# A third high-part buffer, split expert loads and a split down product in a fused time-mix and mixture-of-experts kernel

## The reference

```python
x = x + attn_ref(layernorm(x), ...)       # T = 2048 rows, H = 512
#   v = xln @ Wv; r = sigmoid(mix @ Wr); vmix = sum_t v*dec; x2 = x + r*(vmix @ Wo + bo)
#   kc = square(relu(shift(xc) @ Wck)); vc = kc @ Wcv; out = x2 + sigmoid(xc @ Wcr) * vc
x = x + ffn_ref(layernorm(x), ...)
#   scores = sigmoid(h @ gate_w); group-limited top 4 of 32 experts; weights normalised, times 2.5
#   up = einsum('th,ehi->tei', h, Wu); act = square(relu(up))          # EI = 256
#   routed = einsum('tei,te,eih->th', act, combine, Wd)
#   shared = square(relu(h @ Wsu)) @ Wsd                               # SI = 1024
```

## Time and profile before

| | |
|---|---|
| runs | 1074.92, 1075.74, 1079.47 us; median 1075.74 |
| profiled execution | 1076.93 us, of which the span of the instructions is 1075.0 us |
| busy share of the span | TensorE 98%, VectorE 54%, ScalarE 50%, GpSimd 41% |
| stage 4 | 705 to 1025 us of the span |
| DMA | 186.64 MB, mean 174 GB/s |

### The profile page before, as it was taken

How to read it: one execution, slowest core, us unless ns; L and a number is a source line. 1 busy time by engine, 2 the same in 40 slices (tenths; PEclk the granted TensorE clock), 3 DMA queues, 4 the chain that set the end, 5 groups by cost and what they waited for, 6 DMA issues and landing times.

```text
span 1075.0 us, 17201 instructions
## 1 busy us (share of the span) xinstructions
PE 1056.3 (98%) x4896; PEld 844.7 (79%) x4897; DVE 576.1 (54%) x1113; ACT 535.3 (50%) x893; POOL 438.9 (41%) x327
## 2 busy tenths in 40 slices
PE   7999999999999999999999999999999999999998
PEld 3456888888788878887887888888888887888887
DVE  7987947804670476140025796935545444455514
ACT  5553645333333333333335433367777776777752
POOL 1031304221221122111214423478677777888642
PEclk9999999999999999999999999999999999999999
DMA  8605296416421643234366681168977899788657
GB/s 276 235 1 196 89 341 215 163 57 252 157 96 49 247 156 98 98 118 157 98 224 204 233 289 40 46 170 166 277 178 206 222 229 301 171 159 171 84 193 285
DMA packets 97602, 186.64 MB, mean 174 GB/s; under 512 B 15496, under 2 KB 34952, under 8 KB 97168
## 3 DMA queue, kind: packets, MB, share of 16 engines
q1 hardware_dynamic: 78304, 150.58, 40.4%
q0 software_dynamic: 18816, 34.64, 16.9%
q10 hardware_dynamic: 432, 0.79, 0.3%
HBM read 137.78 MB, written 58.98 MB: 183 GB/s over the span
## 4 chain that ended last, share of the span: by engine, by line
PE 79%; DMA 6%; DVE 6%; issue 4%; POOL 2%; ACT 1%; POOLq 0%; DVEq 0%; ACTq 0%; SPq 0%
PE bank L630 37%; PE bank L952 24%; PE bank L1556 8%; PE bank L534 5%; DMA shx_d<-yo,idy 3%; DMA res_d<-yo,idy 3%; PE bank L1548 2%; PE bank L1564 1%; PE bank L963 1%; POOL xg L1727 1%; PE bank L973 1%; PE bank L1020 1%; DVE bns L317 1%; DVE bns L247 0%; POOL mix_lo L371 0%
## 5 line engine op out<-in xcount | busy, mean ns | idle before, releaser
L933 POOL TENSOR_TENSOR ksp_lo<-ra,ksp_hi 128x512 fp32r<-128x512 f32 x96 | 145.8, 1519 | 443.9 <-ACT ksp_hi L883 443.8
L1700 DVE TENSOR_TENSOR wds<-w,wds 128x1024 fp32r<-128x1024 f32 x84 | 103.1, 1227 | 158.3 <-ACT wds L1637 106.2
L1556 PE MATMUL bank<-w,xT 128*128 x672 | 158.8, 379 | 1.1 <-ACT xT L1621 0.8
L952 PE MATMUL bank<-vring,ksp_hi 128*128 128x512 f32 x512 | 159.4, 393 | 0.0
L875 ACT ACTIVATE ra<-bank 128x512 f32<-128x512 f32 x96 | 57.4, 598 | 175.6 <-PE bank L630 171.2
L1556 PEld LDWEIGHTS bank<-w,xT 128*128 128x128 f32 x672 | 126.9, 189 | 21.5 <-issue 1.8
L630 PE MATMUL bank<-wds,aT 128*128 128x512 f32 x504 | 137.2, 407 | 0.1
L883 ACT ACTIVATE ksp_hi<-ra 128x512 fp32r<-128x512 f32 x96 | 60.7, 632 | 124.6 <-PE bank L952 124.1
L952 PEld LDWEIGHTS bank<-vring,ksp_hi 128*128 128x128 f32 x512 | 95.5, 188 | 20.1
L630 PE MATMUL bank<-xcT_hi,wck_lo 128*128 128x512 f32 x256 | 101.7, 397 | 0.0
L630 PE MATMUL bank<-xcT_lo,wck_hi 128*128 128x512 f32 x256 | 101.5, 396 | 0.0
(11 more groups left out here) (272 smaller groups left out, 1931.4 us busy)
## 6 DMA issues: line engine op xcount, KB each, us to landing
vring<-wcv_d SPq DMA_DIRECT2D x64, 512.0 KB, 3.3
w<-in_L_ffn_Wu SPq DMA_DIRECT2D x32, 512.0 KB
w<-in_L_ffn_Wd SPq DMA_DIRECT2D x32, 512.0 KB
hT_d<-hT SPq DMA_DIRECT2D x16, 512.0 KB, 3.9
hTb<-hT_d SPq DMA_DIRECT2D x3, 2048.0 KB
raw_wcv<-in_L_attn_Wcv SPq DMA_DIRECT2D x4, 1024.0 KB, 7.1
raw_wck<-in_L_attn_Wck SPq DMA_DIRECT2D x4, 1024.0 KB, 10.0
f<-in_L_attn_x SPq DMA_DIRECT2D x4, 1024.0 KB, 6.9
```

What stands on the lines that cost most here:

```text
L933: nc.gpsimd.tensor_tensor(ksp[1][:, i % 2], ra[:, i % 2], ksp[0][:, i % 2], ALU.subtract).then_inc(sem("klo_in"), 1)
L952: m = nc.tensor.matmul(bank[to + j][:], ksp[l][:, i % 2, j * P:(j + 1) * P], rhs(r), start=i == 0 and k == 0, stop=i == last and k == 2)
L1556: m = nc.tensor.matmul(bank[4 + u][:, 0:EI], xT4[:, u, c * P:(c + 1) * P], slot_of(wu8[:, :, c * EI:(c + 1) * EI], e), start=c == 0, stop= ...
L1700: nc.vector.tensor_tensor(wds[:, u, 1], slot_of(wd8, e), wds[:, u, 0], ALU.subtract).then_inc(sem("wl4"), 1)
```

## The change

The high part of the down weights gets three buffers, the low part keeps two, in five separate tensors; the third high part lies where `ksp`'s low part lies in stages 2, 3 and 5. `wd_parts(t)` picks them by the tile's place in its pass. In ScalarE's step `w_hi` stands ahead of `take_y` and waits for the down of tile g-3. `w_lo` waits for the down of tile g-2 and for `w_hi`. The parts of tile 1 are made behind `a_hi` of tile 0, on both engines. `load` is cut in two: `load_up` (Wu) when the expert's last up is done (`u4`), `load_down` (Wd) when its last down is done. At `TH_AT`, row tiles 0 and 1 of the down product of piece 1 come ahead of the wait for the normalised rows, and row tiles 2 and 3 behind the transposes of chunks 0 and 1.

```diff
--- before.py
+++ after.py
@@ -204,7 +204,8 @@
         a4 = at("a4", [P, 2, EI], F, 92.75)
         aT4 = at("aT4", [P, 2, 2, EI], R, 164.5)
         yo = at("yo", [P, YRING, H], F, 172.5)
-        wds = at("wds", [P, 2, 2, EI // P * H], R, 64)
+        wd_hi = [at(f"wd_hi{n}", [P, EI // P * H], R, kb) for n, kb in enumerate((72, 64, 168.5))]
+        wd_lo = [at(f"wd_lo{n}", [P, EI // P * H], R, kb) for n, kb in enumerate((68, 76))]
         idc = at("idc", [P, GROUP], I32, 199.5)
         idy = at("idy", [P, GROUP], I32, 199.625)
 
@@ -944,16 +945,16 @@
             split_product(bank[kc + i % 2][:], lambda s, c: weights[s][:, c, i * P:(i + 1) * P],
                           rhs, C).then_inc(sem("kc_in"), 1)
 
-        def pe_inner_down(pe, n, i, last, rhs, to=0):
+        def pe_inner_down(pe, n, i, last, rhs, to=0, rows=range(BT)):
 
             pe.wait_ge(sem("klo_in"), n + 3)
-            for j in range(BT):
+            for j in rows:
                 for k, (l, r) in enumerate(((0, 0), (0, 1), (1, 0))):
                     m = nc.tensor.matmul(bank[to + j][:], ksp[l][:, i % 2, j * P:(j + 1) * P], rhs(r),
                                          start=i == 0 and k == 0, stop=i == last and k == 2)
                 if to and i == last:
                     m.then_inc(sem("sum3"), 1)
-            if not (to and i == last):
+            if not (to and i == last) and rows[-1] == BT - 1:
                 m.then_inc(sem("vc_done"), 1)
 
         def pe_logits(pe, b, c):
@@ -980,14 +981,16 @@
                 pe.wait_ge(sem("sg_in"), b + 1)
             up(i)
             if router and i == TH_AT:
+                down(i - 2, range(BT // 2))
                 pe.wait_ge(sem("h_in"), b * BT + BT)
                 pe.wait_ge(sem("rc_in"), rc_done)
                 pe_turn_norm(pe, b, 0)
                 pe_turn_norm(pe, b, 1)
+                down(i - 2, range(BT // 2, BT))
             if router and i == TH_AT + 1:
                 pe_logits(pe, b, 2)
                 pe_logits(pe, b, 3)
-            if i >= 2:
+            if i >= 2 and not (router and i == TH_AT):
                 down(i - 2)
             if router and i == TH_AT:
                 pe.wait_ge(sem("kc_free"), n + 3)
@@ -1030,11 +1033,11 @@
                 split_product(bank[6 + j % 2][:], lambda s, c: xcT[s][:, c, 1 + j * P:1 + (j + 1) * P],
                               lambda s, c: wcr[s][:, c], C).then_inc(sem("rcp_in"), 1)
 
-            def down(i):
+            def down(i, rows=range(BT)):
                 if i == 0:
                     pe.wait_ge(sem("u_in"), b * BT + 4)
                 pe.wait_ge(sem(f"vr_in{i % 4}"), 64 * b + 16 * (i // 4) + 16)
-                pe_inner_down(pe, b * NCI + i, i, NCI - 1, lambda s: vring[:, i % 4, s * H:(s + 1) * H])
+                pe_inner_down(pe, b * NCI + i, i, NCI - 1, lambda s: vring[:, i % 4, s * H:(s + 1) * H], rows=rows)
 
             def up(i):
                 if first and i % 4 == 0:
@@ -1122,14 +1125,14 @@
         def pe_block3(pe, b, router=False, between={}):
             pe.wait_ge(sem("hb_in"), 16 * b + 16)
 
-            def down(i):
+            def down(i, rows=range(BT)):
                 if i == 0:
                     if b == 0:
                         pe.wait_ge(sem("u_in"), NB * BT + 4)
                     else:
                         pe.wait_ge(sem("sh_in"), b * BT)
                 pe.wait_ge(sem(f"wsd_lo{i // 4}"), i % 4 // 2 + 1)
-                pe_inner_down(pe, N3 + b * NSI + i, i, NSI - 1, lambda s: wsd[s][:, i])
+                pe_inner_down(pe, N3 + b * NSI + i, i, NSI - 1, lambda s: wsd[s][:, i], rows=rows)
 
             rhs = lambda s, c: hTb[:, bass.ds(b & 1, 1), s, c].rearrange("p a t -> p (a t)")
 
@@ -1264,12 +1267,17 @@
         wu_rows = a["L0_ffn_Wu"].rearrange("e (c p) i -> e p c i", p=P)
         wd_rows = a["L0_ffn_Wd"].rearrange("e (c p) i -> e p c i", p=P)
 
-        def load(sp, e, s):
+        def load_up(sp, e, s):
 
             sp.dma_start(wu8[:, s].rearrange("p (c n) -> p c n", c=C),
                          wu_rows[bass.ds(e, 1)].rearrange("a p c i -> p (a c) i")).then_inc(sem(f"w4_in{s % 4}"), 16)
+        def load_down(sp, e, s):
             sp.dma_start(wd8[:, s].rearrange("p (c n) -> p c n", n=H),
                          wd_rows[bass.ds(e, 1)].rearrange("a p c i -> p (a c) i")).then_inc(sem(f"w4_in{s % 4}"), 16)
+
+        def load(sp, e, s):
+            load_up(sp, e, s)
+            load_down(sp, e, s)
 
         def landed(sp, r, s):
 
@@ -1533,6 +1541,9 @@
         def slot_of(ring, e):
             return ring[:, bass.ds(e & WSLOTS - 1, 1)].rearrange("p a n -> p (a n)")
 
+        def wd_parts(t):
+            return wd_hi[(t + 1) % 3][:], wd_lo[t % 2][:]
+
         def up3(pe, i):
             pe_inner_up(pe, N4 + i, i, wsu, lambda s, c: hT3[:, s, c], kc=6)
 
@@ -1564,12 +1575,13 @@
                     m = nc.tensor.transpose(bank[2 + u][:, c * P:(c + 1) * P], a4[:, u, c * P:(c + 1) * P], ident[:])
                 m.then_inc(sem("at4"), 1)
 
-            def down(g, u):
+            def down(g, u, t):
+                parts = wd_parts(t)
                 pe.wait_ge(sem("al4"), g + 3)
                 pe.wait_ge(sem("wl4"), g + 1)
                 pe.wait_ge(sem("y4"), g + 1)
                 split_product(bank[u][:], lambda s, c: aT4[:, u, s, c * P:(c + 1) * P],
-                              lambda s, c: wds[:, u, s, c * H:(c + 1) * H], EI // P).then_inc(sem("d4"), 1)
+                              lambda s, c: parts[s][:, c * H:(c + 1) * H], EI // P).then_inc(sem("d4"), 1)
 
             def step(i, t, e, more=True):
                 g, u = GROUP * i + t, t % 2
@@ -1577,7 +1589,7 @@
                 if more:
                     tin(i, t + 2, u)
                 turn(g - 1, 1 - u)
-                down(g - 2, u)
+                down(g - 2, u, t - 2)
 
             down2(NSI - 2)
             pe.wait_ge(sem("owner_in"), 1)
@@ -1605,9 +1617,9 @@
             pe.wait_ge(sem("hb_in"), 16 * (NB - 1 + PIECES))
             turn(final, 1)
             up3(pe, 0)
-            down(final - 1, 0)
+            down(final - 1, 0, GROUP - 2)
             up3(pe, 1)
-            down(final, 1)
+            down(final, 1, GROUP - 1)
             for i in range(2, NSI):
                 up3(pe, i)
                 down3(pe, i - 2)
@@ -1630,11 +1642,12 @@
                 act.wait_ge(sem("d4"), g + 1)
                 nc.scalar.activation(aT4[:, u, 0], bank[2 + u][:, 0:EI], ACT.Copy).then_inc(sem("ah4"), 1)
 
-            def w_hi(g, u, e):
-
-                act.wait_ge(sem("d4"), g + 1)
+            def w_hi(g, t, e):
+
+                if not (isinstance(g, int) and g < 3):
+                    act.wait_ge(sem("d4"), g)
                 wait_apart(act, sem("win"), e + 1)
-                nc.scalar.activation(wds[:, u, 0], slot_of(wd8, e), ACT.Copy).then_inc(sem("wh4"), 1)
+                nc.scalar.activation(wd_parts(t)[0], slot_of(wd8, e), ACT.Copy).then_inc(sem("wh4"), 1)
 
             def take_y(i, t, u, e, first=False):
                 g = GROUP * i + t
@@ -1650,8 +1663,8 @@
                 if more:
                     x_in(g + 2, u)
                 a_hi(g - 1, 1 - u)
+                w_hi(g, t, e)
                 take_y(i, t - 2, u, before, first)
-                w_hi(g, u, e)
 
             act.wait_ge(sem("owner_in"), 1)
             passes = passes_of(act)
@@ -1660,13 +1673,13 @@
             w_hi(0, 0, early[0])
             x_in(0, 0)
             x_in(1, 1)
-            w_hi(1, 1, early[1])
             act_rows3(act, NB - 2)
             relu(0, 0)
             x_in(2, 0)
             relu(1, 1)
             x_in(3, 1)
             a_hi(0, 0)
+            w_hi(1, 1, early[1])
             act.wait_ge(sem("bs_st"), 16 * NB)
             for t in range(2, YRING + 2):
                 step(0, t, early[t - 2], early[t], first=True)
@@ -1695,29 +1708,31 @@
                 nc.vector.tensor_tensor(aT4[:, u, 1], bank[2 + u][:, 0:EI], aT4[:, u, 0],
                                         ALU.subtract).then_inc(sem("al4"), 1)
 
-            def w_lo(g, u, e):
+            def w_lo(g, t, e):
+                hi, lo = wd_parts(t)
+                dve.wait_ge(sem("d4"), g + 1)
                 dve.wait_ge(sem("wh4"), g + 1)
-                nc.vector.tensor_tensor(wds[:, u, 1], slot_of(wd8, e), wds[:, u, 0], ALU.subtract).then_inc(sem("wl4"), 1)
-
-            def step(g, u, e):
-                square4(g, u)
-                a_lo(g - 1, 1 - u)
-                w_lo(g, u, e)
+                nc.vector.tensor_tensor(lo, slot_of(wd8, e), hi, ALU.subtract).then_inc(sem("wl4"), 1)
+
+            def step(g, t, e):
+                square4(g, t % 2)
+                a_lo(g - 1, 1 - t % 2)
+                w_lo(g, t, e)
 
             dve.wait_ge(sem("owner_in"), 1)
             passes = passes_of(dve)
             early = first_owners(dve, 2)
             w_lo(0, 0, early[0])
-            w_lo(1, 1, early[1])
             square4(0, 0)
```

(11 more changed lines are left out.)

## The result

| | before | changed |
|---|---|---|
| runs of the first comparison | 1074.92 to 1079.47 us, median of five 1078.74 | 1071.11 to 1073.46 us, median of six 1072.6 |
| ratio to before, 95% interval | 1 | 0.9947 [0.9928, 0.9966] |
| the same, repeated later (35 and 12 runs) | 1073.72 to 1081.59 us, median 1077.39 | 1070.68 to 1074.02 us, median 1072.32, ratio 0.9951 [0.9937, 0.9966] |
| profiled execution, its span | 1076.93, 1074.96 us | 1072.30, 1070.54 us |

What follows compares the result with a forecast made beforehand. TensorE is four fifths of the span, so only its waits can be won. Expert steps 4.0, last tiles 0.9, router 1.0 and loads 0 sum to 5.9 us: 1076.93 - 5.9 = 1071.0 us, range 1069.5 to 1075.0.

Steps and rivals of the forecast that it cites:

- the line of 0.5%: Whole kernel: about what a measurement can tell from no change, 1070.4 us; chances faster 0.38, same 0.54.
- The last tiles: End of expert stage: an earlier low part lets the last square finish before TensorE is free; gain 0.9 us.
- the 2.0 us of slack: Expert steps: with the new order a late weighting may be 2.0 us later than now before TensorE notices.
- so between 0 and 1.6 us stay: Steps at 890 to 927 us: delays of at most 5.4 against 3.8 free; 0.8 of 3.2 us taken as staying.
- rival A: Expert stage: scatters' pace is the bound, more slack helps once, 2.0 us instead of 4.0; 1073.0 us; chance 0.20.
- that much later: Undisturbed expert steps: the early high part starts the weighting about 0.25 us later, covered by ScalarE's 0.84 wait; cost nil.
- Wd and the next Wu go out together again, so nothing changes: Expert loads: among neighbouring experts with one tile each, splitting the loads leaves the bursts unchanged; worth taken as 0.
- bounds of 0.8 either way: Expert loads: at most all of the remaining 0.8 us gained, or as much lost; 0 taken.
- the gain of 1.36: Last block's router transposes: half a down product fits into TensorE's 2.40 us idle; gain 1.36 us.
- The charge of 0.1: Router logits: they follow the transposes sooner, so 0.1 us of wait in each of four blocks.
- Rival B: Expert stage: VectorE's low part holds GpSimd, mean scatter issue well over 1.65 us; slower, 1083 us; chance 0.08.
- C: Expert stage: TensorE's lateness comes from the weighting itself and stays; only last tiles and router gain; 1075.0 us; chance 0.10.

Runs made afterwards that it cites:

- e2: Kernel before with only the three high-part buffers and the new order on ScalarE and VectorE; ratio to before 1.0025.
- e13: Changed kernel with two experts' weights, 2 MB, issued together; ratio to before 1.0007, median 1077.76 us.
- e10: Kernel before with three buffers, new order and loads at two moments, router's product left as before; ratio to before 0.9980.
- e3: Kernel before with only the expert loads at two moments; ratio to before 0.9980.
- e4: Kernel before with six output buffers in place of four; ratio to before 1.0008.
- e9: Kernel before with three buffers and new order, low part also waiting for the next tile's ReLU; ratio to before 1.0007.
- e14: Changed kernel without the loads at two moments, so router's half product and new order only; ratio to before 0.9968.
- e1: Kernel before with only the split down product at the router; ratio to before 0.9977.
- e12: Changed kernel without the new order and its three buffers, so router's half product and loads only; ratio to before 0.9966.

## Why the prediction was right, and where it wasn't

The number held: 1071.0 forecast, 1072.3 in the profiled execution and 1072.6 in the median, inside 1069.5 to 1075.0. At 0.53 and 0.49% the two comparisons lie on either side of the line of 0.5%, whose sides had chances of 0.38 and 0.54. **The sum is right and its terms are not**, so the number is right in part by luck. It had 4.0 + 0.9 + 1.0 + 0; the runs give the order, which the first two belong to, 0.0, the router 3.3 and the loads 2.5, each within some 1.3 us.

*Order, 4.9 forecast, 0.0 measured.* The last tiles did as worked out (0.9; 0.79, the idle 0.63 gone). The failed step is the one that turned the 2.0 us of slack into saved waits: "so between 0 and 1.6 us stay". (Its bound is also added up wrongly: 3.2 and 2.6 are 5.8, not 5.4, so up to 2.0 could stay by its own terms.) It took the lateness of the weightings as given and only added what TensorE's stalls had hidden. In fact the lateness was larger: longest 3.0 to 3.8 us in the four kernels with the old order, 4.0 to 5.2 in four of the five profiles with the new one, 28 to 33 late tiles in place of 7 to 24. The fifth, the changed kernel's second profile, has 3 late tiles and no waits. And the scatters came no faster: from tile 11 to tile 57 they start 3.90 us apart before, 3.95 and 3.91 in the two profiles of the changed kernel, 3.93 in e2 and in the changed kernel with six buffers. I read this as rival A's mechanism, "more slack helps once": a TensorE that no longer waits doesn't let the scatters catch up. It fits the rows and is not shown by an experiment of its own. A's 1073.0 is near the result, though it too had given the order 2.0. The 0.0 is the mean over the four combinations; beside both other parts the order gave 1.5 thousandths, 1.6 us, good to some 2 us.

The price of a weighting "that much later", 0.25 us a step, was taken as covered. It isn't there at all: the weighting starts as long behind its down product as before.

*Loads, 0 forecast, 2.5 measured.* The failed step: "Wd and the next Wu go out together again, so nothing changes". They don't: SyncE's rows have them 1.4 to 2.4 us apart in turn, for Wu goes at the end of an up and Wd at the end of a down. Its bounds of 0.8 either way were too narrow as well, since they counted only what the order had left over. That it is the smaller bursts that give the 2.5 rests on e13, where larger ones cost 6.0. The earlier landing count is the smaller matter: TensorE's 0.3 us for it are in three kernels with the old loads and in none with the new.

*Router, 1.0 forecast, 3.3 measured.* The mis-sized term is the gain of 1.36 with nothing beyond it. The trace of the change does what was said: idle 2.40 to 1.07, and 127.15 to 127.21 us from the transposes to the stage's first up in all eight profiles with this part, 128.5 to 128.9 in the six without. But the idle time that the gain was read from is not in every execution. Of the six profiles without this part only two (the kernel before and e10) have it; in e2, e3, e4 and e9 TensorE was done 0.7 to 1.7 us later with the up product ahead of them, having waited 0.6 to 0.7 us for the load of `hTb` near 561, and began them at 575.17 to 576.09 without idle time. That wait is in one of the eight with this part (e14, 0.4). The charge of 0.1 for the logits wasn't needed (low part from 578.38, logits at 579.38, no wait). The first up lies at 704.22 in the mean of the eight, at 704.89 in the six: 0.7. The rest would have to lie in the steps, whose waits are indeed smaller with this part in each pair, in one only just (e1 0.9 against 4.8, e14 2.6 against 5.2, the whole 1.6 and none against 2.6 of e10, e12 2.7 against 2.9). Why the steps should feel it isn't settled; the small differences at the stage's start, from which the lags grow apart, are as far as the traces go.

*Rival B* stated the right hold and the wrong size. The scatters' mean is 1.71 to 1.74, over its mark of 1.65, but the gathers gave back what the scatters lost (1.24 in place of 1.40). The mark also tells the orders apart poorly: e1, e3 and e12, with the old order, have 1.65 to 1.68. Its loss is e2's 2.5 thousandths at most, not 8 us. *C*, that nothing but last tiles and router remains, fits the order's worth in the mean, but not its reason: the high part and the low part did leave the way from the weighting to the down product.

## What to carry to other kernels

Before you book a saved wait, ask what the queue that trails will do with it: here 2.0 us more slack in each step came to nothing in the mean. Loads that nobody waits for can still have a price by the size of their bursts: here 512 KB at two moments was the best of three. An idle time read in one profile may be absent from the next execution; look at a second one before a gain is worked out from it. And where parts of a change touch one loop, try them in all combinations; a right total proves none of its terms.

## What the runs showed of the hardware

GpSimd's issue of an indirect transfer is held when it starts while VectorE's subtraction of the down weights runs, and ends at a fixed time behind it. GpSimd, then VectorE, in the changed kernel:

```profile
996.25 1.32 POOL L1742 DMA_INDIRECT xg<-h_d,idc  x1 [0.30 <-ACT yo L1657]
...
1000.14 1.70 POOL L1763 DMA_INDIRECT shx_d<-yo,idy  x1 [0.69 <-issue]
```

```profile
995.42 1.23 DVE L1715 TENSOR_TENSOR wd_lo<-w,wd_hi 128x1024 fp32r<-128x1024 f32 x1 [0.93 <-ACT wd_hi L1650]
...
999.19 1.23 DVE L1715 TENSOR_TENSOR wd_lo<-w,wd_hi 128x1024 fp32r<-128x1024 f32 x1 [0.93 <-ACT wd_hi L1650]
```

The gather ends 0.92 us behind the subtraction, the scatter 1.42; free, they take 1.05 and 1.58. Over the whole stage of this profile 30 gathers that start inside a subtraction end 0.91 to 0.93 us behind it and 25 scatters 1.41 to 1.51, while the 35 scatters in which a subtraction begins take 1.58 in the middle. So the issue doesn't hold VectorE in turn. VectorE's instructions of this line, shortest, middle and longest in ns:

```profile
L1715 DVE TENSOR_TENSOR wd_lo<-w,wd_hi x84: 1224/1226/1252, 701.3 to 1020.8; 128x1024 fp32r<-128x1024 f32 x84
```

None of the 84 was stretched, though most began inside a running issue. Between an issue of GpSimd's and this subtraction the hold goes one way only.

Where GpSimd computes, it is another matter. Its subtraction for the shared expert's weights (`wsu_lo`) falls beside VectorE's normalised rows (`hb`) in the kernel before, and behind them in e3:

```profile
571.87 4.92 DVE L799 TENSOR_SCALAR hb<-f,bna,nsc 128x512 f32<-128x512 f32 x4
573.98 2.53 POOL L1192 TENSOR_TENSOR wsu_lo<-raw3a,wsu_hi 128x1024 fp32r<-128x1024 f32 x1
576.83 1.23 DVE L1192 TENSOR_TENSOR wsd_lo<-raw3b,wsd_hi 128x1024 fp32r<-128x1024 f32 x1
```

```profile
572.71 2.90 DVE L799 TENSOR_SCALAR hb<-f,bna,nsc 128x512 f32<-128x512 f32 x4
575.28 2.58 POOL L1192 TENSOR_TENSOR wsu_lo<-raw3a,wsu_hi 128x1024 fp32r<-128x1024 f32 x1
575.64 3.30 DVE L1192 TENSOR_TENSOR wsd_lo<-raw3b,wsd_hi 128x1024 fp32r<-128x1024 f32 x1
```

What GpSimd's subtraction meets on VectorE is some 2.0 us longer: the four instructions of `hb` 4.92 for 2.90, or `wsd_lo` 3.30 for 1.23. All fourteen profiles have one or the other (ten the first, e2, e3, e4 and e9 the second). The 2.40 us that TensorE idles for `hb` contain this hold. The Trainium skill, "SBUF — State Buffer", on the two sides of SBUF, has an exclusive lock on a shared pair of ports that whichever engine starts first keeps for the whole instruction; for a VectorE instruction with two inputs in SBUF, as the subtraction of the down weights is, it says so only against a GpSimd instruction that reads SBUF. The trace agrees for GpSimd's subtraction, where VectorE's instruction comes second, and for an issue that comes second to VectorE's subtraction; it disagrees for an issue that comes first. Whether an issue reads SBUF, which the second half of the rule asks, no row here shows.

In the repeated run of the changed kernel the scatters' lag is 4.0 to 5.5 us at tiles 18 to 36, where the first profile stood at 8.0 by tile 30. I take it that a GpSimd with 0.5 us to spare in a step (3.77 less the 3.25 of the earlier trace rows) catches up until its start falls into the subtraction and then keeps that lag, that two executions of one kernel can settle at different lags, and that this makes much of their scatter in time. It was argued from two profiles and not tested.
